# Attention on one core: the value products of three k tiles issued together, six value blocks in a unit in place of eight

## The reference, cut to what matters

```
q = (x @ Wq.T).reshape(b, t, h_kv, g, d).transpose(0, 2, 3, 1, 4)
k = (x @ Wk.T).reshape(b, t, h_kv, d).transpose(0, 2, 1, 3)
v = (x @ Wv.T).reshape(b, t, h_kv, d).transpose(0, 2, 1, 3)
att = jnp.einsum('bhgqd,bhkd->bhgqk', q, k) / jnp.sqrt(d)
att = jax.nn.softmax(att, axis=-1)
y = jnp.einsum('bhgqk,bhkd->bhgqd', att, v)
```

## Time and profile before

| | |
|---|---|
| time, median of three runs | 3494.24 us (3490.64 to 3494.65) |
| the profiled execution's own time | 3492.64 us |
| its span, first to last instruction | 3491.0 us |
| mean granted TensorE clock | 0.996 of full speed |
| PE busy | 3443.2 us, 99% of the span |
| DVE busy | 2211.4 us, 63% |
| ACT busy | 1597.9 us, 46% |
| POOL busy | 1627.0 us, 47% |

### The profile page before, as it was taken

The page is one execution under the profiler, slowest core; times in us unless marked ns, Lnnn a source line. Parts: engine busy times, 40 slices in busy tenths (PEclk is TensorE's granted clock), DMA queues, the critical chain, the costliest instruction groups (busy, mean ns, idle before and its releaser), DMA issues.

```text
span 3491.0 us, 45636 instructions
## 1 busy us (share of the span) xinstructions
PE 3443.2 (99%) x17196; PEld 2303.4 (66%) x17196; DVE 2211.4 (63%) x3722; ACT 1597.9 (46%) x3006; POOL 1627.0 (47%) x712
## 2 busy tenths in 40 slices
PE   7999999999999999999999999999999999999998
PEld 5778555555555555555555388888888888888786
DVE  5545877777777777777777288644444444443727
ACT  3211566666666666666666623322222222214544
POOL 1213789988989988899899800000000000001000
PEclk9999999999999999999999999999999999999999
DMA  6765655656555555555555645511111111113212
GB/s 233 213 193 178 169 107 111 121 109 125 106 121 111 110 119 116 118 111 120 112 104 119 142 155 174 165 30 31 30 30 30 30 30 30 30 42 123 98 62 88
DMA packets 194996, 370.49 MB, mean 106 GB/s; under 512 B 41920, under 2 KB 118976, under 8 KB 174336
## 3 DMA queue, kind: packets, MB, share of 16 engines
q0 software_dynamic: 37408, 203.97, 25.7%
q1 hardware_dynamic: 153952, 157.84, 16.3%
q10 hardware_dynamic: 3456, 6.29, 0.6%
HBM read 168.42 MB, written 64.87 MB: 67 GB/s over the span
## 4 chain that ended last, share of the span: by engine, by line
PE 96%; DVE 1%; DMA 1%; ACT 1%; issue 0%; SPq 0%; POOL 0%; ACTq 0%; DVEq 0%
PE att_scores L1075 16%; PE att_scores_T L1089 14%; PE gu_gate_acc L1656 14%; PE gu_up_acc L1656 14%; PE att_y_acc L1100 14%; PE qkv_qk_acc L595 5%; PE wo_acc L1373 5%; PE down_acc L1954 5%; PE down_acc L1940 5%; PE att_den_acc L790 2%; PE qkv_v_acc L578 1%; PE qkv_mod_acc L523 1%; ACT att_exp L979 0%; PE wo_h_T L1255 0%; ACT qkv_h_affine L335 0%; DMA qkv_wmod_lo<-in_wmod 0%
## 5 line engine op out<-in xcount | busy, mean ns | idle before, releaser
L1008 DVE TENSOR_REDUCE att_chunk_max<-att_scores 128x1 f32<-128x512 f32 x1984 | 1212.1, 680 | 342.3 <-PE att_scores L1075 342.3
L979 ACT ACTIVATE att_exp<-att_scores_T 128x512 f32<-128x512 f32 x2048 | 1049.7, 620 | 443.9 <-PE att_scores_T L1089 423.8
L918 POOL TENSOR_TENSOR att_exp_pair<-att_exp 128x2048 f32<-128x2048 f32 x256 | 1199.1, 4731 | 45.8 <-ACT att_exp L979 39.4
L1100 PE MATMUL att_y_acc<-att_exp,att_v_head 128*32 128x512 f32 x4096 | 497.0, 603 | 0.0
L1520 POOL DMA_DIRECT2D inter_scratch<-gu_inter x84 | 45.2, 538 | 853.9 <-DVE gu_inter L1414 853.9
L1075 PE MATMUL att_scores<-att_kq,att_q_stack 96*128 96x512 f32 x768 | 325.6, 428 | 1.3 <-DVEq L1054 0.7
L1075 PE MATMUL att_scores<-att_k_stack,att_q_stack 96*128 96x512 f32 x768 | 324.9, 426 | 0.4
L1089 PE MATMUL att_scores_T<-att_q_stack,att_k_stack 98*128 98x512 f32 x768 | 299.4, 412 | 2.8 <-ACT att_exp L979 2.3
L1089 PE MATMUL att_scores_T<-att_q_stack,att_kq 98*128 98x512 f32 x768 | 296.7, 406 | 0.7 <-ACT att_exp L979 0.7
L1582 ACT ACTIVATE gu_magnitude<-gu_value 128x512 f32<-128x512 f32 x88 | 55.7, 633 | 525.7 <-DVE gu_value L1614 525.7
L1613 DVE TENSOR_TENSOR gu_rounded<-gu_up_acc,gu_rounded 128x512 f32<-128x512 f32 x88 | 60.9, 692 | 327.0 <-PE gu_up_acc L1656 327.0
(11 more groups left out here) (230 smaller groups left out, 6097.6 us busy)
## 6 DMA issues: line engine op xcount, KB each, us to landing
att_exp_pair<-att_exp_pair POOLq DMA_DIRECT2D x128, 1024.0 KB, 7.1
att_q_stack<-q_scratch SPq DMA_DIRECT2D x72, 256.0 KB, 5.8
shared_raw<-in_wd_t POOLq DMA_DIRECT2D x34, 256.0 KB, 3.1
qkv_x_tile<-in_x SPq DMA_DIRECT2D x16, 512.0 KB, 4.1
q_scratch<-qkv_qk_out_hi POOLq DMA_DIRECT2D x32, 256.0 KB, 3.2
q_scratch<-qkv_qk_out_lo POOLq DMA_DIRECT2D x32, 256.0 KB, 4.7
qkv_wqkv_raw<-in_wmod POOLq DMA_DIRECT2D x8, 1024.0 KB, 7.5
qkv_wmod<-in_wmod POOLq DMA_DIRECT2D x8, 1024.0 KB, 8.5
```

Source lines behind the costliest of these rows:

```text
L918: nc.gpsimd.tensor_tensor(ps[PAIR_SLOT[j]][:], pr[2 * j % NP][:], pr[(2 * j + 1) % NP][:], ALU.add).then_inc(pair_done, 1)
L979: nc.scalar.activation(pr[k % NP][:, h * NB:(h + 1) * NB], stp[bank_of(u, c, GH * k + h)][:], ACT.Exp, scale=INV_SQRT_DH).then_inc(exp_don ...
L1008: nc.vector.reduce_max(cmax[c % 2][:, q:q + 1], turn_buffer(u, c, q)[:], AX.X).then_inc(sm_done, steps_done(u, q))
L1100: ins = nc.tensor.matmul(yp[h * DH:(h + 1) * DH, :], vg[c // QB % 2][:, k, :], pr[k % NP][:, h * NB:(h + 1) * NB], start=(k == 0), stop=(k ...
```

## The change

The value blocks come in k tiles 0, 3, 6, 9, 12 and 14. Those at 3, 6, 9 and 12 hold three k tiles, those at 14 and 0 hold two. A k tile without a block uses the order that odd k tiles had. The second denominators move from k tile 2 to k tile 3. Every matmul, reduction, exponential, copy and DMA is still there and there are as many as before; what changes is the order on TensorE.

```
-    DEN_AT = (0, 2, 6)
+    DEN_AT = (0, 3, 6)
+    BY_V = {0: (14, 15), 3: (0, 1, 2), 6: (3, 4, 5), 9: (6, 7, 8), 12: (9, 10, 11), 14: (12, 13)}
...
-                    if k % 2:
+                    if k not in BY_V:
                         for h in range(GH):
                             ahead_turn()
                             scores_t(u, c, k, h)
...
-                    for b in (2, 1):
+                    for n in BY_V[k]:
                         if k > 0:
-                            by_v(u, c, g, k - b)
+                            by_v(u, c, g, n)
                         elif not is_first(u):
-                            by_v(u - 1, (c - 1) % BODY, g, KT - b)
+                            by_v(u - 1, (c - 1) % BODY, g, n)
```

## The result

| | before | after |
|---|---|---|
| median | 3494.44 us (3490.64 to 3498.35, 4 runs) | 3532.83 us (3531.59 to 3533.55, 4 runs) |
| ratio to before | | 1.0111, 95% interval 1.0098 to 1.0124 |
| span of the profiled execution | 3491.0 | 3531.9 |

The change makes the kernel 1.1% slower. The forecast was 3521 in a range of 3511 to 3532: the right way, but 38 us of loss where the sum said 28, and just outside the range.

The account below looks back on a forecast made before the run. PE's order of issue was taken to bound the kernel. 30 middle units +26.7, first unit +1.1 and last +0.2 gave +28 us on 3492.64, so 3520.6; with the median 1.6 above that execution, 3521 was forecast, range 3511 to 3532.

Parts of the forecast that it names:

- What bounds the kernel: Whole kernel: PE, busy 99% of the span, sets the time by its order of issue; its starts show it, not waits.
- Part 1: Value blocks on PE: entering and leaving one costs about 0.38 us, so two fewer in a unit give back about 0.8.
- Part 2: Four long stretches a unit: twelve turns wait for DVE's reductions through three banks, 6.47 us each, a hold of 0.43.
- The spare 0.05: Stretches of eight turns before the change: they just fit DVE's pace, 3.67 us by the rule against 3.72 measured.
- Part 3: Other work in a unit: the reciprocal's 0.10 us goes; denominators, buffers, ACT, POOL and SP add no loss.
- First unit: First unit of the attention stage: long stretches hold 15 turns, +0.27 us for three k tiles, four times, +1.1.
- Last unit: Last unit, without turns, ACT the clock: +0.1 to +0.3 us in all, 4 either way from blocks at the lower clock.
- The sum: One middle unit, block to block: blocks -0.26 and stretches +1.15 give +0.89 us, +26.7 for 30 units.
- A: Rival on long stretches: the ring doesn't hold, 6.04 us each, unit -0.83, time about 3468; 8 in 100.
- B: Rival on long stretches: hold about as large as the saving, 6.25 us each, time 3487 to 3501; 4 in 100.
- C: Rival on held turns: they cost PE more than the wait, stretch up to 6.7 us, time over 3533; 5 in 100.

## Why the prediction was right or wrong

- **What bounds the kernel: right.** The loss is in the order on PE, and shows in its starts only.
- **Part 1, what a block costs: roughly right.** 0.38 forecast; 0.35 with the two-bank ring, 0.26 with short reductions. The step of 0.39 into a block, which the forecast put down to the block, holds some 0.06 of waiting: with short reductions it is 0.33. The 0.241 for a step of PE was a mean over a stretch with such waits in it, too; unheld it is 0.235 or less.
- **Part 2, the long stretch: right in its mechanism, a little short in size.** 6.47 forecast, 6.49 to 6.50 measured, because the block follows a held turn by 0.43 and not 0.41. Four of them are 25.97 in place of 25.88, 2.8 us in 30 units. The runs with short reductions show that it is DVE's pace, the runs with seven blocks that it grows as worked out. The spare 0.05 of a stretch of eight turns was really a hold of 0.06. The stretch from k tile 14 to 0 has nine turns, not eight; as it has nine before and after, nothing hangs on it.
- **Part 3, what moves with the change: this is the step that failed.** It went through the reciprocal, the denominators, the buffers, POOL and SP, and said of ACT that in a held stretch it has more room. It left out ACT's cast of the output weights in k tile 2 of units 2 to 9, so a term of 5.4 us stood at nothing. The cast's cover, the block of k tile 2, was taken away: 8 x 0.68 = 5.4 us, as moving the cast back ahead of a block shows. What it said of the reciprocal held: the stretch with it is no longer than the others now.
- **First unit: right.** From the stage's first matmul to the first transpose it takes 49.8 before and 50.9 after, +1.1 as forecast (15 turns in 8.29, 8.28 forecast). The other 2.5 us up to that transpose lie ahead of the stage, which begins at 363.9 before and 366.4 after with the same code ahead of it. They go with the granted clock, 0.99 of full speed in the one record and 0.97 in the other (the first two rows below). Of the twelve profiles of this study the three that begin the stage at 363.6 to 364.0 have 10 us at the lower level ahead of it, the other nine, at 365.3 to 367.2, have 17 us or more.
- **Last unit:** +1.9, within the 4 either way that I gave. Four value blocks fall on the lower level in place of three; they take 5.6 us more than at the full clock where the three took 4.4 more, so 1.2 of it is the clock. The 1.3 us behind the attention stage go with the clock as well: it falls once more for 3.4 us just behind that stage, which it doesn't before (the last two rows, 56 us from the start of the output projection). In the twelve profiles the part from there to the end takes 1486.1 and 1486.9 without such a fall and 1487.5 to 1489.4 with one. Whether the new order had a part in these falls stays open.

```profile
20.00:363.00 343.00, 325.86 (x1709) 256.42 (x1708) 187.68 (x337) 74.46 (x178) 77.15 (x119) 0.99 0.63 194
20.00:363.00 343.00, 326.87 (x1698) 256.61 (x1698) 186.79 (x336) 74.77 (x178) 75.96 (x116) 0.97 0.63 194
2004.80:2060.80 56.00, 55.83 (x268) 44.30 (x269) 47.81 (x70) 12.45 (x31) 8.90 (x3) 1.00 0.52 159
2044.40:2100.40 56.00, 55.85 (x261) 44.13 (x262) 42.76 (x68) 12.38 (x31) 11.52 (x4) 0.97 0.54 160
```

- **The sum:** the middle unit grew by 1.14 us where 0.89 was forecast, so 30 units by 34.1 where 26.7 was forecast; 5.4 of the difference is the cast and 2.8 the long stretch, and small shifts elsewhere take 0.8 back. The rest of the 12 us lies before and behind those units, and nearly all of it goes with the clock. With the cast moved, the kernel is inside the range at 3527.
- **Rivals.** A (the ring doesn't hold, the change only saves) fell: the ring holds. The saving that it counted on exists, but is smaller than its 0.83 a unit: with DVE's hold gone undisturbed units are 0.5 shorter with six blocks, and of that nothing is left in the medians, since other chains come next. B fell, the hold is twice what the saving is. C fell: held turns cost nothing beyond DVE's 0.60.

## What to carry to other kernels

A block of other work in a loop is also the time in which the consumers catch up. Where a consumer needs longer for one item than the producer (here 0.60 against 0.47) and the ring between them is short, fewer and longer blocks can cost more than the switches that they save. Work out for each item of a stretch when its slot in the ring comes free (here 1.27 us for the fourth item and 0.60 more for each one behind it) and when the producer gets there; from the first item for which the slot is later, the consumer is the clock until the next block. And when a block is moved, list everything that any engine queues ahead of its old place, the rare things of a few iterations too: what was free there may not be free in the middle of a stretch.

## What the runs showed of the hardware that I had not expected

A PSUM bank that goes from TensorE to ACT and back is tied up for 1.18 us, with an exponential whose own distance on ACT is 0.48: with two banks in place of three the kernel with eight blocks was 5.6% slower, the one with six 4.4% slower than the same kernel with three. For turns and DVE the round with an idle DVE is 0.54 + 0.73 = 1.27 us, where reductions start 0.60 apart. In both, the round is more than twice the consumer's distance, so the number of banks has to be worked out from the round and not from an engine's pace.
